# Attention stage: another order of steps on GpSimd

## What is computed

```python
xn = layernorm(x)
# attention: 16 heads of 16, keys j with i - 128 <= j <= i
q, k, v = xn @ Wq.T + bq, xn @ Wk.T + bk, xn @ Wv.T + bv
attn = softmax(where(mask, q @ k.T / 4, -10000.0)) + 1e-9
a = (attn @ v) @ Wo.T + bo
# feed-forward: 8 experts of 256x512x256, 2 per token, and one shared expert
logits = xn @ gate_w.T
idx = top_k(logits + beta, 2); c = sigmoid(logits[idx])
h = silu(xn @ gate_proj[e]) * (xn @ up_proj[e]); eo = h @ down_proj[e]
f = sum over idx of c * eo[idx]  +  the same with the shared weights
out = x + a + f
```

## Time and profile before

| | us |
|---|---|
| median of 3 runs | 1711.3 (1709.48 to 1714.91) |
| span of the profiled execution | 1707.4 |
| PE busy in it | 1539.4 (90%) |
| POOL busy | 1105.5 (65%) |
| DVE busy | 1106.2 (65%) |
| ACT busy | 985.4 (58%) |

### The profile page before, as it was taken

The page is one execution under the profiler, slowest core; times in us unless marked ns, Lnnn a source line. Parts: engine busy times, 40 slices in busy tenths (PEclk is TensorE's granted clock), DMA queues, the critical chain, the costliest instruction groups (busy, mean ns, idle before and its releaser), DMA issues.

```text
span 1707.4 us, 38917 instructions
## 1 busy us (share of the span) xinstructions
PE 1539.4 (90%) x11382; PEld 1267.9 (74%) x11382; DVE 1106.2 (65%) x3788; ACT 985.4 (58%) x2043; POOL 1105.5 (65%) x1158
## 2 busy tenths in 40 slices
PE   4888869999999999999998898888998989888897
PEld 4677748999998888889996566666766666666665
DVE  7898866666666666666667566666666666666642
ACT  5677745455545455544554566666666665666663
POOL 1877774443334443334432689989888888988888
PEclk9899989999999999999996799999999999999999
DMA  6777755555555555555655677676777676667642
GB/s 189 260 267 254 272 198 187 159 173 162 163 160 160 159 167 164 162 159 160 187 184 134 149 167 158 129 157 157 164 152 175 151 168 153 149 137 156 163 121 82
DMA packets 228581, 288.89 MB, mean 169 GB/s; under 512 B 59488, under 2 KB 146144, under 8 KB 228512
## 3 DMA queue, kind: packets, MB, share of 16 engines
q1 hardware_dynamic: 170064, 207.30, 44.2%
q10 hardware_dynamic: 45488, 45.36, 9.3%
q0 software_dynamic: 12960, 35.41, 8.3%
HBM read 198.07 MB, written 79.95 MB: 163 GB/s over the span
## 4 chain that ended last, share of the span: by engine, by line
PE 43%; POOL 30%; issue 15%; DVE 8%; ACT 2%; ACTq 1%; POOLq 1%; DMA 1%; DVEq 0%
PE psum L152 25%; PE psum L961 11%; POOL plain_arena L1441 5%; POOL plain_arena L1439 5%; POOL plain_arena L1466 4%; POOL plain_arena L1479 3%; POOL split_arena L1458 3%; POOL plain_arena L1473 2%; POOL plain_arena L408 2%; PE psum L1518 2%; PE psum L1148 2%; POOL plain_arena L411 2%; PE psum L1560 1%; POOL split_arena L1453 1%; POOL plain_arena L1449 1%
## 5 line engine op out<-in xcount | busy, mean ns | idle before, releaser
L152 PE MATMUL psum<-split_arena 128*128 128x512 f32 (+2 forms) x4752 | 946.4, 352 | 11.5 <-DVE split_arena L1252 4.2
L152 PEld LDWEIGHTS psum<-split_arena 128*128 128x128 f32 x4752 | 757.5, 194 | 133.9 <-issue 24.9
L1791 DVE CUSTOM_DVE_ANT_0 plain_arena<-psum,mask 128x256 f32<-128x256 f32 (+1 forms) x1024 | 338.6, 385 | 234.9 <-PE psum L1518 214.6
L1675 ACT ACTIVATE plain_arena<-psum 128x512 f32<-128x512 f32 (+1 forms) x512 | 250.3, 542 | 231.4 <-PE psum L1541 188.2
L1111 POOL TENSOR_TENSOR split_arena<-plain_arena,split_arena 128x1024 fp32r<-128x1024 f32 x43 | 103.3, 2402 | 228.1 <-ACT split_arena L1183 227.8
L1217 ACT ACTIVATE plain_arena<-psum 128x512 f32<-128x512 f32 (+1 forms) x172 | 90.2, 524 | 250.2 <-PE psum L152 218.5
L961 PE MATMUL psum<-split_arena 128*128 128x256 f32 x1704 | 218.1, 286 | 3.5 <-DVE split_arena L1282 3.5
L961 PEld LDWEIGHTS psum<-split_arena 128*128 128x128 f32 x1704 | 208.1, 191 | 5.8 <-DVE split_arena L1282 4.1
L1287 DVE TENSOR_TENSOR plain_arena<-psum,plain_arena 128x512 f32<-128x512 f32 (+1 forms) x172 | 102.5, 596 | 140.0 <-ACT plain_arena L1217 90.3
L1103 POOL DMA_INDIRECT plain_arena<-xn_d,run_ix x142 | 136.7, 963 | 69.4 <-POOL run_ix L1100 35.2
L1439 POOL TENSOR_SCALAR_AFFINE_SELECT plain_arena<-plain_arena 128x1024 f32<-128x1024 f32 x128 | 140.4, 1097 | 36.6 <-ACT plain_arena L1675 35.7
(11 more groups left out here) (199 smaller groups left out, 1890.8 us busy)
## 6 DMA issues: line engine op xcount, KB each, us to landing
plain_arena<-in_gate_w SPq DMA_DIRECT2D x43, 512.0 KB, 3.4
plain_arena<-in_up_w SPq DMA_DIRECT2D x43, 512.0 KB
plain_arena<-in_down_w SPq DMA_DIRECT2D x43, 512.0 KB
plain_arena<-in_x SPq DMA_DIRECT2D x32, 512.0 KB, 6.9
q_d<-split_arena SPq DMA_DIRECT2D x32, 512.0 KB, 3.2
k_d<-split_arena SPq DMA_DIRECT2D x32, 512.0 KB, 4.9
split_arena<-q_d SPq DMA_DIRECT2D x128, 128.0 KB, 3.7
split_arena<-k_d SPq DMA_DIRECT2D x128, 128.0 KB, 3.9
```

The source lines that it names most:

```text
L152: last = pe.matmul(out, lhs_t(p), rhs(q), start=(begins and c == 0 and k == 0), stop=(ends and c == len(chunks) - 1 and k == 2), skip_grou ...
L1675: act.activation(b_pt[:, g % 2, 2 * p + par, 4 * half:4 * half + n, :].rearrange("p k s -> p (k s)"), psum[:, 2 + par, 0:n * P], ACT.Exp, ...
L1791: last = dve.tensor_tensor_reduce(b_junk[:, 2 * par + i % 2, 0:cols], psum[:, par, at:at + cols], mask[:, 2 * P - cols:2 * P], -1.0, 3e38, ...
```

## The change

Only POOL's order in the third stage changes. The lower parts of hidden chunks 0, 1, 2 go from h = 11, 13, 15 to h = 12, 14 and h = 0 of the next turn, that of chunk 3 from h = 1 to h = 2; in these half pairs they stand behind the selects. The bias additions go from h = 12 and 14 to h = 13 and 15. The two routed additions of the first half of the rows go from h = 0 and 1 to h = 15 of the turn before, behind the second bias addition; those of the second half go from h = 2 and 3 to h = 3 and 5. The wait of the first gather (h = 4) asks for two counts of `b_f` less, and the fifth gather (h = 8) gets a wait for the rest.

```diff
             def gather(b, k):
                 half, a, n = k // 4, k // 2, k % 2
+                if k % 4 == 0 and not is_first(b):
+                    hold(pool, b_f, 6 * b - 2 + 2 * half)
                 if k == 0:
-                    pool.wait_ge(b_f, 6 * b) if not is_first(b) else None
                     hold(pool, b_stg, b + 1)
...
-                    b, m = chunk_due(t, h)
+                    b, m = chunk_due(t, h - 1) if h > 0 else chunk_due(t - 1, H - 1)
                     if b is not None:
                         hidden_lo(b, m)
-                    if h < 4 and valid(t - 2):
-                        add_routed(t - 2, h // 2, h % 2)
+                    if h in (3, 5) and valid(t - 2):
+                        add_routed(t - 2, 1, (h - 3) // 2)
                     if 4 <= h < 12 and valid(t - 1):
                         gather(t - 1, h - 4)
-                    if h in (12, 14) and valid(t - 1):
-                        add_bias(t - 1, (h - 12) // 2)
+                    if h in (13, 15) and valid(t - 1):
+                        add_bias(t - 1, (h - 13) // 2)
+                    if h == 15 and valid(t - 1):
+                        for n in range(2):
+                            add_routed(t - 1, 0, n)
```

## The result

| | before | changed |
|---|---|---|
| median of the runs, us | 1710.8 (4 runs) | 1668.1 (4 runs, 1662.6 to 1670.5) |
| ratio, 95% interval | | 0.9737 (0.9723 to 0.9752) |
| span of the profiled execution | 1707.4 | 1668.8 |

The change makes the kernel 42.7 us faster. The forecast was 1661 us in a range of 1653 to 1692. The profiled execution was the slowest of the four (1670.5 us); a second trace of the same kernel comes with the experiments (e9).

What follows compares the result with a forecast made beforehand. POOL was taken to set the pace, waiting through its own order. Fourteen turns of 44.35 us (PE) instead of 47.69 save 46.8 us, 50.2 with the ends: span 1657.2, plus 3.9 gives 1661 us, range 1653 to 1692.

Steps and rivals of the forecast that it cites:

- POOL's waits were the loss: Attention stage: POOL sets the pace, and 3 to 4.7 us of each turn are waits at hidden_lo that go.
- PE sets the next bound, 44.35 us a turn: Attention turns: without waits on POOL, PE needs 44.35 us against POOL's 44.0, so PE sets the turn.
- the clock drops stay: Rival, chance 0.25: PE's clock still drops every second turn, turns of 44.35 and 45.95 us, mean 45.15, 1672 us.
- The additions' move: POOL around the turn's end: bias and routed additions change places; two fewer stand between h=0 and h=4 (2.5 us).
- The cost ahead of the select of h=0: POOL at the turn's end: four steps take 5.08 us, 0.5 more than before, but start 2.26 us earlier.
- The clock: PE's drop to 1.2 GHz in longer turns was taken to go with the second gap; this decides 11 us.
- the wait of 1.68 us: PE's wait on POOL's select of h=4, ahead of the values at h=6, forecast to go.
- the forecast's gap of 0.92 us: First of two close PE gaps before the clock drop; it stays, an argument for the drops staying.
- SP's and ACT's queues keep their order: DMA queues of SP and ACT: order unchanged by the moves; no time was added for it.
- ACT takes POOL's place: Rival, chance 0.14: PE's waits on exponentials and at the maxima double, 26.7 us come back, 1688 us.

Runs made afterwards that it cites:

- e9: The changed kernel itself, run and traced once more, against the kernel before: 1666.2 us, ratio 0.9741.
- e1: The kernel before with only the lower parts of the hidden chunks moved, bias and routed additions left in place: 1670.5 us, ratio 0.9761.
- e4: The changed kernel with one more 128x512 addition on POOL in each turn, into a buffer nobody reads: 1671.7 us, ratio 0.9769.
- e6: The changed kernel without POOL's two bias additions a turn, so bo is left out of the result: 1663.2 us, ratio 0.9717.
- e3: The changed kernel with SyncE's 512 KB load of the normalised rows issued at h = 13 instead of h = 8: 1662.4 us, ratio 0.9720.
- e10: A repeat of the changed kernel with the normalised rows' load at h = 13 instead of h = 8: 1662.5 us, ratio 0.9725.
- e8: The changed kernel with rows' load at h = 13, result's store from SyncE's queue, and sums' DMA issues behind the next exponentials: 1703.7 us, ratio 0.9965.
- e11: The kernel before with only the lower parts moved and the rows' load at h = 13, no addition moved: 1667.4 us, ratio 0.9749.
- e12: The changed kernel with rows' load at h = 13 and sums' DMA issues behind the next exponentials, store not moved: 1698.1 us, ratio 0.9907.
- e5: The changed kernel with the 512 KB result's store issued from SyncE's queue instead of ScalarE's, rows' load still at h = 8: 1671.5 us, ratio 0.9781.

## Why the prediction was right, and where it was off

**POOL's waits were the loss.** Right: e1 moves only the step that POOL waited at, and brings 40 of 43 us.

**PE sets the next bound, 44.35 us a turn.** Right for the turns in which nothing else is late: 44.36 measured. The waits left in it are there: 11.6 us for exponentials and 12.2 at the maxima, 13.8 and 12.9 before. By e4's step count POOL has 0.5 us of room, and e6 shows that taking work from it shortens no turn. The mean of all fourteen turns, 45.17 us, is by chance that of the rival "the clock drops stay" (45.15); its mechanism, a drop in every second turn, isn't there.

**The additions' move.** The cost ahead of the select of h=0 was right (5.11 against 5.08), and so was it that the values don't wait for the selects there. The forecast gave the move no gain; 2 to 5 us are likely but not clear of noise. What the forecast missed is how much hangs on the other move: with hidden_lo at its old place the same move costs 59 us.

**The clock.** Right for the reason given. The drop, which half of the fourteen turns had before, is gone with the wait of 1.68 us, and a whole turn shows 1.00 throughout. In the fourteen turns of the changed kernel's first trace it comes back only behind PE's waits of 2.3 and 3.3 us, in e9 behind one of 1.55. Of the two sections of the Trainium skill (TensorE: Matmul & The Clock Gate), the trace agrees with "HAM oscillation — how this bites in real kernels" in that the drops stood behind a wait of the loop and went with it, but not in that each pass has one: the wait of 1.68 us was in all fourteen turns, the drop in seven. What "A second HAM failure mode: psum-queue depth-cycling" says is not seen here, though a turn still has gaps of 0.79, 0.87 and 0.27 us, the second of them the forecast's gap of 0.92 us (ahead of the maxima transpose, at 1331.92 us in the trace before).

**What was off: 7 us in the median, 11.6 in the profiled span** (1668.8 against 1657.2). That execution was the slowest of its four. By places: the 14 turns took 632.3 us instead of 620.9, of which 4.5 are in the first and 5.6 in the last, and 1.3 in others; ahead of them 1.7 us more than forecast, behind them 1.5 less. In e9, the same kernel, the 14 turns took 626.2.

The step that failed is "SP's and ACT's queues keep their order", behind which the forecast put the landing of transfers at nothing. The order is kept, but the turn is 7% shorter and the transfers of h=8 to 13 (store, two loads of 512 KB, gathers, keys) are as large as before. PE's waits at the transposed scores for a DMA or with no releaser were 1.4 us before (976 to 1610 us, none over 0.5). They are 11.6 in the changed kernel and 7.0 in e9, and 2.3 and 1.8 with one 512 KB load moved away (e3, e10), whose spans are 1658.1 and 1660.8 against 1668.8 and 1664.5. That the crowd of transfers makes the 8 KB late is argued from this and not shown for each landing: in e10 the one of the first turn still took 8.12 us. Why that turn suffers most stays open; it was over 46 us in all kernels with the later lower parts except e3, e8 and e11, and 46.85 in the kernel before, like its others.

The rival "ACT takes POOL's place" had the wrong agent. PE's waits on ACT didn't grow; waits at the transposed scores that no engine ended took 10 of the 27 us which it foresaw (5.6 in e9). With ScalarE's issues moved too (e8, e12), the waits on DMAs are far larger, but that edit also has a cost of its own, as said.

The fastest kernel of the study that computes the whole layer is e3 (again e10), at 1662.4 us, 0.972 of the kernel before.

## What to carry to other kernels

When two engines are both at nine tenths, subtract from the turn of each the waits that it has on the other; the larger rest is the next bound. Here it gave the length of the undisturbed turns to 0.01 us, and the time of the kernel to 7 us. A step that an in-order engine does sooner than anyone needs it makes its wait a wait of all that stands behind it, so put it behind what is urgent, and do this before filling the time: the same additions seem worth 2 to 5 us after that move and cost 59 us without it. After a gain of some per cent look at small DMAs that gate an engine: the turn is shorter, and the large transfers beside them are as large as before.

## What the runs showed of the hardware

The 8 KB of the maxima, issued while a store and a load of 512 KB and gathers were under way, landed after 8.07 and 8.88 us in the first and last turn of the changed kernel (DMA share 1.02 and 0.99 meanwhile), and after 7.43 and 7.14 in e9. With the 512 KB load issued elsewhere the first landing took 7.33 us in e3 and 8.12 in e10. With the store in the other engine's queue PE still waited 1.79 us in the first turn (e5).

A single wait of PE of 1.26 us at 1157 us in the changed kernel left the granted clock at 1.00 in the 4 us behind it; behind one of 1.55 us in e9 the 4 us from 1022 were at 0.69, and behind those of 2.28 and 3.26 us in the changed kernel at 0.50, the lower level of 1.2 GHz.
